# Post-norm decoder layer, experts: from all experts on all tokens to sorted blocks through one expert each, with the sorting done beside the cross attention

## The chip, the core and the metric

The kernel runs on one core of a Trainium2 chip. The metric is the time of one execution on the device, in microseconds (us); lower is better. A core has TensorE (PE in the rows; PEld is its load of stationary operands), VectorE (DVE), ScalarE (ACT), GpSimd (POOL) and SyncE (SP), which run their own instruction streams and meet at semaphores. Matrix results land in PSUM, everything else on the core lies in SBUF.

## The reference

64 sequences of 128 tokens, width 128; a context of 64 x 120 x 128. Three sublayers, each followed by `x = layernorm(x + sublayer(x))`:

```python
# 1 linear attention, 16 heads of 8, softplus features, cumulative sums over the sequence
# 2 cross attention, 16 heads of 64: latents x ask context and latents (120 + 128 keys)
q = lat @ Wq;  k, v = split(concat([layer_norm(ctx), lat]) @ Wkv)
out = softmax(q k^T / 8) v @ Wout
# 3 experts
scores = softmax(x @ gate_w.T)                     # 8 experts
topk_w, topk_i = top_k(scores, 2)
topk_w = topk_w / (topk_w.sum(-1) + 1e-20) * 2.5
g = silu(x @ w_gate[e]) * (x @ w_up[e])            # every e, F = 176
y = sum_e combine[t, e] * (g @ w_down[e])          # combine is 0 but for the two chosen
return y + (silu(x @ sw_gate) * (x @ sw_up)) @ sw_down   # shared, F = 352
```

So the two chosen of eight experts decide a token's result, and the shared part takes every token.

## The kernel before, in words

Three stages follow each other, each in a block of its own with an instruction stream per engine; everything is unrolled. `X` in SBUF (128 positions x 64 sequences x 128) carries the layer's rows from stage to stage. A product that needs more than one pass of precision is a `split_product` (L493): each operand is split into a high and a low part of type float32r, and three matmuls (hi x lo, lo x hi, hi x hi; L496, L497, L498) add up in PSUM. Transposes and the matmuls of L937 and L926 are plain float32, which the trace shows as two records each where it is a matmul and as one where it is a transpose.

**Cross attention** (`cross_attention`, L501) goes in 32 rounds of two sequences, 16 units a round; a unit `s` is two heads of one sequence. TensorE's order in unit `s` is: transpose the probabilities of unit `s` (L962), scores of unit `s+3` (L496 to L498 into `ps_S`), in even units the product `G` for a later pair, in odd ones a tile of values `V`, and every fourth unit the weighted values of four units (L937, "gang"). In unit 2 it also makes the output projection of the round before (L926). The chain of one unit is: scores, maximum (VectorE L793), exponentials (ScalarE L735), reciprocal (VectorE L799, in `inverse`), scaling of the probabilities (GpSimd L660, in `weights`), transpose (TensorE L962), copy (ScalarE L743). VectorE's order in unit `s` is `V_copy` in even units, `G_lo` (L779) in odd ones, `out_copy` in every fourth, then `maxima(s+3)` and `inverse(s+2)`. GpSimd scales unit `s+2` and puts small things between: deviation, normalisation (L652) and the copy into `X` (L655) of the round before, and key and context work. Ahead of the first round GpSimd builds a 0/1 matrix `spread`, and between the scaling of units 1 and 2 it splits the experts' and the shared gate and up weights (L703, L705).

**Experts** (`experts`, L1023) takes 16 groups of 512 tokens. The 8 x 176 expert columns and the 352 shared ones are 14 blocks of 128 (11 and 3), each a gate and an up `split_product` over 512 tokens; 11 `spread_weights` matmuls (L1332) turn the token's eight weights into a factor per expert column, and 14 `split_product`s with `down` add up `ps_y`. ScalarE makes silu (L1179) and the high part of `hidden` (L1168), VectorE the products (L1264, L1270) and the routing, 21 small operations a group (L1224 to L1247), GpSimd the low part (L1124) and the last normalisation (L1138 to L1145).

## Time and profile before

| | |
|---|---|
| median of 3 runs | 2255.25 us (2255.05 to 2255.89) |
| the profiled execution | 2259.26 us, its span 2257.3 us |
| linear attention, 0 to 311 us | not touched but for semaphore names |
| set-up of cross attention | 311 to 338.1 us |
| 32 rounds | 338.1 to 1674.6 us |
| experts | 1687.4 to 2257.3 us |
| busy share of the span | PE 96%, DVE 69%, ACT 62%, POOL 61% |
| mean granted clock of TensorE | 0.983 of full |

A row of the busy time by stage has the stretch, its length, then for PE, PEld, DVE, ACT and POOL the busy time with the number of instructions, the granted clock, the share of the DMA engines, and GB/s. TensorE's matmuls are pipelined: one takes 0.28 to 0.40 us from start to end, and the next starts before it ends, so throughput is read from the distance of the starts. In a timeline the bracket behind an instruction is the idle time of its engine before it and who ended it.

### The profile page before, as it was taken

What the parts mean: (1) busy time and instruction counts of PE and PEld (TensorE: products, weight loads), DVE (VectorE), ACT (ScalarE), POOL (GpSimd) and SP (SyncE); (2) the same over time, 40 slices, a digit from 0 to 9 for tenths busy, and PEclk for the clock granted to TensorE, in tenths of its full rate; (3) what the DMA queues carried; (4) which work ended last, traced back from release to release, by engine and by line L of the source; (5) the groups of instructions that cost most, each with busy time, mean ns of one, the idle gap of its engine ahead of it and who ended that gap; (6) DMA issues with size and microseconds to landing.
All of it is one profiled execution on the core that took longest, in us unless ns stands there. A gap on an engine that the chain in (4) does not pass through costs nothing. (4 is left out here: it accounts for less than half of the span.)

```text
span 2257.3 us, 44552 instructions
## 1 busy us (share of the span) xinstructions
PE 2164.8 (96%) x16235; PEld 1847.5 (82%) x16235; DVE 1548.4 (69%) x3425; ACT 1395.0 (62%) x3756; POOL 1372.0 (61%) x1481
## 2 busy tenths in 40 slices
PE   6899968999999999999999999999989999999998
PEld 3555547999999999999999999999977777777776
DVE  3799955666666666666666666666657777777775
ACT  3455535666666676666766666666745665665664
POOL 4688846565565665655655656656644666666666
PEclk9999979999999999999999999999999999999999
DMA  3311100000000000000000000000000000000000
GB/s 100 111 34 32 32 24 6 11 6 6 11 6 6 11 6 9 8 6 11 6 6 10 6 6 10 6 6 10 6 1 1 10 5 10 10 6 11 10 6 15
DMA packets 52794, 33.40 MB, mean 15 GB/s; under 512 B 3096, under 2 KB 50274, under 8 KB 52450
## 3 DMA queue, kind: packets, MB, share of 16 engines
q1 hardware_dynamic: 50174, 26.30, 4.0%
q10 hardware_dynamic: 2404, 4.26, 0.7%
q8 instruction: 131, 2.15, 0.4%
q14 instruction: 85, 0.70, 0.1%
HBM read 22.16 MB, written 8.39 MB: 14 GB/s over the span
## 5 line engine op out<-in xcount | busy, mean ns | idle before, releaser
L660 POOL TENSOR_TENSOR x_prob<-x_prob,x_inv 128x496 f32<-128x496 f32 x514 | 520.8, 1013 | 548.9 <-DVE x_inv L799 548.8
L735 ACT ACTIVATE x_prob<-x_ps_S,x_nmax 128x248 f32<-128x248 f32 x1028 | 473.3, 467 | 131.0 <-DVE x_nmax L793 131.0
L793 DVE TENSOR_REDUCE x_nmax<-x_ps_S 128x2 f32<-128x496 f32 x515 | 345.5, 671 | 182.8 <-PE x_ps_S L498 182.5
L743 ACT COPY x_probT<-x_ps_T 124x512 f32<-124x512 f32 x512 | 300.4, 587 | 226.3 <-PE x_ps_T L962 226.3
L1124 POOL TENSOR_TENSOR e_hidden_lo<-e_hidden,e_hidden_hi 128x512 fp32r<-128x512 f32 x224 | 291.2, 1303 | 198.4 <-ACT e_hidden_hi L1168 197.6
L496 PE MATMUL x_ps_S<-x_kT_lo,x_G_hi 128*128 128x248 f32 x1030 | 329.8, 320 | 0.0
L962 PE MATMUL x_ps_T<-ident,x_prob 128*124 128x128 f32 x2048 | 314.8, 276 | 11.7 <-POOL x_prob L660 11.7
L962 PEld LDWEIGHTS x_ps_T<-ident,x_prob 128*124 128x124 f32 x2048 | 237.6, 139 | 72.0 <-POOL x_prob L660 29.5
L497 PE MATMUL x_ps_S<-x_kT_hi,x_G_lo 128*128 128x248 f32 x1030 | 287.2, 279 | 0.0
L498 PE MATMUL x_ps_S<-x_kT_hi,x_G_hi 128*128 128x248 f32 x1030 | 286.8, 278 | 0.0
L779 DVE TENSOR_TENSOR x_G_lo<-x_ps_G,x_G_hi 128x512 fp32r<-128x512 f32 x259 | 178.8, 690 | 130.0 <-ACT x_G_hi L729 129.9
L937 PE MATMUL x_ps_O<-x_probT,x_V 124*64 124x128 f32 x4096 | 251.8, 276 | 0.2 <-ACT x_probT L743 0.2
L937 PEld LDWEIGHTS x_ps_O<-x_probT,x_V 124*64 124x64 f32 x4096 | 221.0, 137 | 18.9 <-issue 5.1
L1179 ACT ACTIVATE e_silu<-e_ps_gate 128x512 f32<-128x512 f32 x224 | 134.5, 601 | 155.7 <-PE e_ps_gate L498 150.3
L729 ACT CAST x_G_hi<-x_ps_G 128x512 fp32r<-128x512 f32 x259 | 152.0, 587 | 91.8 <-PE x_ps_G L498 91.8
L735 ACT ACTIVATION_READ_ACCUMULATOR x_prob<-x_ps_S,x_nmax 128x1 f32 x1028 | 206.5, 201 | 0.0
L497 PEld LDWEIGHTS x_ps_S<-x_kT_hi,x_G_lo 128*128 128x128 f32 x1030 | 196.4, 191 | 0.0
L496 PEld LDWEIGHTS x_ps_S<-x_kT_lo,x_G_hi 128*128 128x128 f32 x1030 | 195.6, 190 | 0.0
L498 PEld LDWEIGHTS x_ps_S<-x_kT_hi,x_G_hi 128*128 128x128 f32 x1030 | 194.9, 189 | 0.0
L1264 DVE TENSOR_TENSOR e_act_up<-e_silu,e_ps_up 128x512 f32<-128x512 f32 x176 | 120.3, 684 | 90.7 <-PE e_ps_up L498 52.7
L785 DVE COPY x_V<-x_ps_V 124x512 f32<-124x512 f32 x259 | 176.7, 682 | 2.3 <-PE x_ps_V L498 2.3
L282 POOL TENSOR_TENSOR lin_kv<-lin_qk,lin_v 128x1024 f32<-128x1024 f32 x64 | 135.1, 2129 | 32.8 <-issue 22.0
(199 smaller groups left out, 5015.4 us busy)
## 6 DMA issues: line engine op xcount, KB each, us to landing
x_nk<-latents SPq DMA_DIRECT2D x34, 124.0 KB
lin_x_rows<-in_x SPq DMA_DIRECT2D x32, 128.0 KB, 2.3
latents<-lin_nlat SPq DMA_DIRECT2D x32, 128.0 KB, 1.8
out_dram<-e_result SPq DMA_DIRECT2D x16, 256.0 KB, 2.2
x_nk<-in_ctx SPq DMA_DIRECT2D x34, 120.0 KB, 2.2
w_wkv<-in_L_xattn_Wkv SPq DMA_DIRECT2D x1, 1024.0 KB, 6.2
w_rows<-in_L_ffn_w_gate SPq DMA_DIRECT2D x1, 704.0 KB, 5.9
w_rows<-in_L_ffn_w_up SPq DMA_DIRECT2D x1, 704.0 KB, 6.2
```

Of the source, the lines that this page charges most:

```text
L496: nc.tensor.matmul(out, stationary[0], moving[1], start=first, stop=False)
L497: nc.tensor.matmul(out, stationary[1], moving[0], start=False, stop=False)
L498: return nc.tensor.matmul(out, stationary[0], moving[0], start=False, stop=last)
L660: nc.gpsimd.tensor_tensor(prob[:, k], prob[:, k], inv[:, k].unsqueeze(2).broadcast_to([P, 2, K]), ALU.mult).then_inc(prob_ready, 1)
L735: nc.scalar.activation(prob[:, k, h, :], ps_S[:, n % BANKS, h * K:(h + 1) * K], ACT.Exp, bias=nmax[:, k, h:h + 1], accum_out=total[:, k, h ...
L743: nc.scalar.copy(probT[0:KT, s % (2 * GANG)], ps_T[0:KT, s % 2, :]).then_inc(probT_ready, 1)
L779: nc.vector.tensor_tensor(G_part[1][:, pair].rearrange("p h u q -> p (h u q)"), ps_G[:], G_part[0][:, pair].bitcast(F32).rearrange("p h u ...
L785: nc.vector.tensor_copy(V[:, hf, u, tile, :], ps_V[0:KT, :]).then_inc(V_ready, 1)
L793: nc.vector.tensor_reduce(nmax[:, k, :], ps_S[:, n % BANKS, 0:2 * K].rearrange("p (h k) -> p h k", h=2), AX, ALU.max, negate=True).then_in ...
L937: last = nc.tensor.matmul(ps_O[h * DH:(h + 1) * DH, k * S:(k + 1) * S], V[:, j // 4, u, tile, (j % 4 * 2 + h) * DH:(j % 4 * 2 + h + 1) * D ...
L962: last = nc.tensor.transpose(ps_T[0:KT, s % 2, at:at + S], prob[:, s % RINGS, h, tile * KT:(tile + 1) * KT], ident[:])
L1124: nc.gpsimd.tensor_tensor(hidden_part[1][0:rows, n % RING, :], hidden[0:rows, n % 2, :], hidden_part[0][0:rows, n % RING, :].bitcast(F32), ...
```

## The change

Only the experts that a token has chosen are computed for it.

During the cross attention, each round also handles the two finished sequences of the round before: TensorE transposes their rows (`turn_rows`) and makes logits (`logits`, plain float32); VectorE works out choice, weights and place in 25 small steps (`route`), spread over units 11, 13, 14 and 15 and over units 0, 3 and 6 of the next round; TensorE counts ranks within the expert with triangular and all-ones matrices (`ranks`, 4 small matmuls) in unit 2 of the next round; GpSimd copies the rows twice into a staging buffer with their number (`keep`, `twin`) and sends both copies by four indirect DMAs (`scatter`) to the place of their expert in a DRAM array. The transposed rows go to DRAM too. The split of the expert weights moves into the units of round 0.

The experts stage then runs over 2 x 71 blocks of 128 sorted rows (16384 rows and room for an incomplete block of each expert in both halves): a block is loaded from DRAM at a row read from a table, transposed, split, taken through gate and up of one expert (one `split_product` with 352 moving columns), multiplied by its weights, transposed, taken through `down` in plain float32, and scattered by an indirect DMA to the rows' own places in a second DRAM array. Twelve row buffers are waited for in sets of three. TensorE puts the shared part of 16 groups between the blocks, eight pieces a group; two groups go ahead of the blocks. The two results of a token are loaded back, eight groups beside the second half's blocks and eight behind the last, added to `X`, and normalised. The number of an expert is read into a register of TensorE for each block, the row of a block into one of SyncE.

Its core (a line of "..." stands where lines are left out):

```diff
+BATCHES = 2
+PER = B // BATCHES
+REGION = PER * S + P
+BLOCKS = (2 * PER * S + EXPERTS * (P - 1)) // P
+SPARE = BLOCKS - 2 * PER * S // P
+BATCH_ROWS = EXPERTS * REGION + SPARE * P
+CLOSERS = BATCHES * (EXPERTS + SPARE)
+WIDTH = D + 4
...
+            def twin(n):
+
+                nc.gpsimd.tensor_copy(staged[:, n % 2, 1, :, 0:D], staged[:, n % 2, 0, :, 0:D]).then_inc(twin_ready, 1)
+                nc.gpsimd.tensor_copy(staged[:, n % 2, :, :, D].bitcast(U32), ids[:, :, n * 2:n * 2 + 2]
+                                      ).then_inc(twin_ready, 1)
+
+            def scatter(n, c, u):
+
+                pool.wait_ge(twin_ready, n * 2 + 2)
+                pool.wait_ge(routed, (n + 1) * STEPS)
+                nc.gpsimd.indirect_dma_start(slots.rows, bass.IndirectOffsetOnAxis(slot[:, n % 2, c, u:u + 1], 0),
+                                             staged[:, n % 2, c, u, :], None).then_inc(slots.scattered[n % 2], 16)
...
-                        deviation(r - 1, s - 4)
-                    if s == 6:
+                    if s in (1, 3) and r > 2:
+                        scatter(r - 3, 1, s // 2)
+                    if s == 4 and r:
+                        deviation(r - 1)
+                    if s in (5, 6) and r:
+                        normalise(r - 1, s - 5)
+                    if s > 13 and r > 1:
+                        scatter(r - 2, 0, s - 14)
+                    if s == 7:
                         keys_hi(r + 1, 1 - par)
-                    if s == 7:
+                    if s == 8:
                         keys_lo(r + 1, 1 - par)
-                    if later_round(r) and s in (8, 9):
-                        normalise(r - 1, s - 8)
-                    if s == 10:
+                    if s == 9 and r:
+                        keep(r - 1)
+                    if s == 10 and r:
+                        twin(r - 1)
+                    if s == 11:
                         context_deviation(r + 2)
-                    if s in (11, 12):
-                        normalise_context(r + 2, par, s - 11)
+                    if s in (12, 13):
+                        normalise_context(r + 2, par, s - 12)
...
+            nc.gpsimd.iota(ids[:], [[B * S, 2], [S, B]], base=0, channel_multiplier=1).then_inc(set_ready, 1)
+            nc.gpsimd.memset(ones[:].bitcast(F32), 1.0).then_inc(set_ready, 1)
+            nc.gpsimd.memset(picked[:].bitcast(F32), 0.0).then_inc(set_ready, 1)
+            for e in range(EXPERTS):
+                nc.gpsimd.memset(index[:, e:e + 1], float(e)).then_inc(set_ready, 1)
+                for n in range(BATCHES):
+                    nc.gpsimd.memset(slots.base[:, n, e:e + 1], float(n * BATCH_ROWS + e * REGION)).then_inc(set_ready, 1)
+            nc.gpsimd.tensor_tensor(before[:], tri[:], ident[:], ALU.subtract).then_inc(set_ready, 1)
             for k in range(2):
                 weights(k, k)
...
             rounds(pool, body)
+            last = ROUNDS - 1
             for u in range(2):
-                deviation(ROUNDS - 1, u)
-                normalise(ROUNDS - 1, u)
-            pool.wait_ge(part_ready, 4)
-            pool.wait_ge(spread_ready, 1)
+                scatter(last - 2, 1, u)
+            for k in range(4):
+                scatter(last - 1, k // 2, k % 2)
+            deviation(last)
+            for u in range(2):
+                normalise(last, u)
+            keep(last)
+            twin(last)
+            for k in range(4):
+                scatter(last, k // 2, k % 2)
...
+            ROUTE = {11: (0, 2), 13: (2, 6), 14: (6, 11), 15: (11, 16)}
+            ROUTE_LATE = {0: (16, 20), 3: (20, 22), 6: (22, STEPS)}
...
+            pe.wait_ge(wT_ready, 5)
+            pe.wait_ge(set_ready, SETS)
...
+            def turn_rows(n):
+
+                pe.wait_ge(staged_ready, n * 2 + 2)
+                pe.wait_ge(outT_ready, min((n + 1) * GANGS + 2, ROUNDS * GANGS))
+                for u in range(2):
+                    last = nc.tensor.transpose(ps_O[:, u * S:(u + 1) * S], staged[:, n % 2, 0, u, 0:D], ident[:])
+                last.then_inc(xT_psum, 1)
+
+            def logits(n):
+
+                pe.wait_ge(xT_ready, n + 1)
+                for u in range(2):
+                    last = nc.tensor.matmul(ps_O[:, 2 * S + u * EXPERTS:2 * S + (u + 1) * EXPERTS],
+                                            xT[:, n % 2, u * S:(u + 1) * S], gwT[:], start=True, stop=True)
+                last.then_inc(logit_psum, 1)
+
+            def ranks(n):
+
+                pe.wait_ge(routed, n * STEPS + 15)
+                pe.wait_ge(outT_ready, min((n + 2) * GANGS, ROUNDS * GANGS))
+                flat = picked[:].rearrange("p k e -> p (k e)")
+                at = 3 * S
+                nc.tensor.matmul(ps_O[:, at:at + 2 * EXPERTS], before[:], flat[:, EXPERTS:3 * EXPERTS], start=True, stop=False)
+                nc.tensor.matmul(ps_O[:, at:at + 2 * EXPERTS], ones[:], flat[:, 0:2 * EXPERTS], start=False, stop=True)
+                at += 2 * EXPERTS
+                nc.tensor.matmul(ps_O[:, at:at + EXPERTS], ones[:], flat[:, EXPERTS:2 * EXPERTS], start=True, stop=False)
+                nc.tensor.matmul(ps_O[:, at:at + EXPERTS], ones[:], flat[:, 2 * EXPERTS:3 * EXPERTS], start=False, stop=True
+                                 ).then_inc(rank_psum, 1)
...
                     if s % GANG == 0 and unit + s:
+                        if s == 12 and r:
+                            pe.wait_ge(shifted_ready, r)
+                        if s == 4 and r > 1:
+                            pe.wait_ge(routed, (r - 2) * STEPS + 22)
                         gang_output(r * GANGS + s // GANG - 1)
+                    if s == 2 and r > 1:
+                        ranks(r - 2)
 
```

The experts stage, new functions (GpSimd, VectorE, SyncE and TensorE):

```diff
+            def load_rows(q):
+
+                if q >= LOADS:
+                    sp.wait_ge(sent[(q - LOADS) % SENDS], through(q - LOADS, SENDS))
+                for i in range(q * SET, min((q + 1) * SET, TOTAL)):
+                    if i == BLOCKS:
+                        sp.wait_ge(tails_stored[1], (EXPERTS + 1) * 16)
+                    row = sp.value_load(entry(row_of, i), min_val=0, max_val=BATCHES * BATCH_ROWS - P)
+                    sp.dma_start(x_rows[:, i % RING, :], slots.rows[bass.ds(row, P), :]).then_inc(rows_loaded[q % LOADS], 16)
...
+            def scatter(i):
+
+                pool.wait_ge(y_ready, i + 1)
+                nc.gpsimd.indirect_dma_start(slots.results,
+                                             bass.IndirectOffsetOnAxis(x_rows[:, i % RING, D:D + 1].bitcast(mybir.dt.uint32), 0),
+                                             y[:, i % (SET * SENDS), :], None).then_inc(sent[i // SET % SENDS], 16)
+
+            def add_pair(g):
+
+                pool.wait_ge(back_loaded[g % BACKS], (g // BACKS + 1) * 32)
+                nc.gpsimd.tensor_tensor(back[:, g % BACKS, 0], back[:, g % BACKS, 0], back[:, g % BACKS, 1], ALU.add
+                                        ).then_inc(pair_ready, 1)
...
+            for t in range(TOTAL + 4):
+                i = t - 3
+                if 0 <= i < TOTAL:
+                    scatter(i)
+                for delay, what in ((0, add_pair), (3, deviation)):
+                    g = back_at(t, delay)
+                    if g is not None:
+                        what(g)
+            for g in range(BACK, GROUPS):
+                add_pair(g)
+                if g > BACK:
+                    deviation(g - 1)
+            deviation(GROUPS - 1)
 
...
+            sent_after(act, TOTAL)
+            for g in range(BACK, BACK + BACKS):
+                load_back(act, g)
+            for g in range(BACK, GROUPS):
+                if g + BACKS < GROUPS:
+                    load_back(act, g + BACKS)
+                normalise(g)
...
+            def take(i):
+
+                dve.wait_ge(y_psum, i + 1)
+                if i % SET == 0 and i >= SET * SENDS:
+                    q = i // SET - SENDS
+                    dve.wait_ge(sent[q % SENDS], through(q, SENDS))
+                v.tensor_copy(y[:, i % (SET * SENDS), :], ps_y[:, 0:D]).then_inc(y_ready, 1)
...
+            def gate_up(i, e):
+
+                pe.wait_ge(lo_ready, i + 1)
+                wait(pe, hidden_ready, i - 1)
+                split_product(nc, ps_gu[:, i % 2, 0:2 * F], [x[:, i % 2, :] for x in xT_part],
+                              [w[:, bass.ds(e, 1), :, :].rearrange("p o n f -> p (o n f)") for w in later.gate_up]
+                              ).then_inc(gu_psum, 1)
...
+            def project_down(i, e):
+
+                pe.wait_ge(hT_ready, i + 1)
+                wait(pe, y_ready, i)
+                for n in range(2):
+                    last = nc.tensor.matmul(ps_y[:, 0:D], hT[:, i % 2, n * P:(n + 1) * P],
+                                            later.down[:, bass.ds(e, 1), n, :].rearrange("p o d -> p (o d)"),
+                                            start=(n == 0), stop=(n == 1))
+                last.then_inc(y_psum, 1)
+
+            def shared(g, k):
+
+                if k < NS:
+                    n, rows = g * NS + k, rows_of[k]
+                    if k == 0:
+                        pe.wait_ge(all_lo_ready, g + 1)
+                    moving = [x[:, g % 2, :] for x in all_part]
+                    wait(pe, all_silu_ready, n)
+                    split_product(nc, ps_gate[0:rows, :], [w[:, k * P:k * P + rows] for w in later.shared[0]], moving
+                                  ).then_inc(gate_psum, 1)
+                    wait(pe, all_hidden_ready, n)
+                    split_product(nc, ps_up[0:rows, :], [w[:, k * P:k * P + rows] for w in later.shared[1]], moving
+                                  ).then_inc(up_psum, 1)
+                elif k < NS + GROUP:
+                    q = k - NS
+                    if q == 0:
+                        pe.wait_ge(all_hidden_ready, (g + 1) * NS)
+                        wait(pe, added, g)
+                    for n in range(NS):
                         rows = rows_of[n]
...
+            for t in range(TOTAL + 4):
+                if t < TOTAL:
+                    turn_rows(t)
+                if 0 <= t - 1 < TOTAL:
+                    gate_up(t - 1, expert[t - 1])
+                g, k = shared_at(t)
+                if g is not None:
+                    shared(g, k)
+                if t + 1 < TOTAL:
+                    expert[t + 1] = pe.value_load(entry(expert_of, t + 1), min_val=0, max_val=EXPERTS - 1)
+                if 0 <= t - 2 < TOTAL:
+                    turn_hidden(t - 2)
+                if 0 <= t - 3 < TOTAL:
+                    project_down(t - 3, expert.pop(t - 3))
 
 
```

## Rows read from the trace of the kernel before

**Rows 1.** Busy time by stage: set-up, rounds, end of cross attention, experts.
```profile
311.00:338.10 27.10, 21.30 (x100) 17.71 (x100) 13.06 (x27) 10.01 (x24) 14.15 (x17) 0.65 0.11 29
338.10:1674.60 1336.50, 1327.04 (x12608) 1236.52 (x12608) 875.72 (x2009) 898.01 (x2814) 775.27 (x956) 1.00 0.03 7
1674.60:1687.40 12.80, 5.78 (x64) 5.37 (x64) 1.88 (x6) 0.00 (x0) 4.76 (x10) 0.91 0.00 1
1687.40:2257.30 569.90, 553.71 (x2497) 435.94 (x2497) 417.99 (x931) 333.56 (x562) 362.73 (x330) 0.98 0.03 8
```

**Rows 2.** Waits from 400 to 1600 us: who waited for whom, total, times, longest.
```profile
POOL x_prob L660 <- DVE x_inv L799: 493.8, 319, 4.4
...
PEld x_ps_T L962 <- POOL x_prob L660: 15.9, 87, 0.2
```

**Rows 3.** Timeline of TensorE, part of a round: start, length, instruction.
```profile
1051.06 0.60 PE L962 MATMUL x_ps_T<-ident,x_prob 128*124 128x128 f32 x4
1051.42 0.36 PE L496 MATMUL x_ps_S<-x_kT_lo,x_G_hi 128*128 128x248 f32 x1
...
1052.19 0.28 PE L496 MATMUL x_ps_G<-x_kT_lo,x_M_hi 128*128 128x256 f32 x1
...
1052.99 1.97 PE L937 MATMUL x_ps_O<-x_probT,x_V 124*64 124x128 f32 x32
1054.89 0.66 PE L962 MATMUL x_ps_T<-ident,x_prob 128*124 128x128 f32 x4
...
1056.07 0.39 PE L496 MATMUL x_ps_V<-x_wv_lo,x_kT_hi 128*124 128x512 f32 x1
1056.30 0.39 PE L497 MATMUL x_ps_V<-x_wv_hi,x_kT_lo 128*124 128x512 f32 x1
...
1058.60 3.73 PE L926 MATMUL x_ps_V<-w_wo,x_outT 128*128 128x128 f32 x32
1062.17 0.60 PE L962 MATMUL x_ps_T<-ident,x_prob 128*124 128x128 f32 x4
```

**Rows 4.** Timeline of VectorE in the same round.
```profile
1047.60 0.69 DVE L785 COPY x_V<-x_ps_V 124x512 f32<-124x512 f32 x1
1048.73 0.68 DVE L793 TENSOR_REDUCE x_nmax<-x_ps_S 128x2 f32<-128x496 f32 x1 [0.43 <-PE x_ps_S L498]
...
1050.06 0.69 DVE L779 TENSOR_TENSOR x_G_lo<-x_ps_G,x_G_hi 128x512 fp32r<-128x512 f32 x1 [0.59 <-ACT x_G_hi L729]
```

**Rows 5.** Timeline of GpSimd in the same round.
```profile
1049.55 1.02 POOL L660 TENSOR_TENSOR x_prob<-x_prob,x_inv 128x496 f32<-128x496 f32 x1 [0.80 <-DVE x_inv L799]
1051.48 1.01 POOL L660 TENSOR_TENSOR x_prob<-x_prob,x_inv 128x496 f32<-128x496 f32 x1 [0.92 <-DVE x_inv L799]
```

**Rows 6.** Groups by line and form, 1700 to 2257 us: busy, mean ns, idle before.
```profile
L1124 POOL TENSOR_TENSOR e_hidden_lo<-e_hidden,e_hidden_hi 128x512 fp32r<-128x512 f32 x208 | 268.8, 1295 | 186.9 <-ACT e_hidden_hi L1168 186.1
...
L1179 ACT ACTIVATE e_silu<-e_ps_gate 128x512 f32<-128x512 f32 x207 | 124.4, 601 | 140.1 <-PE e_ps_gate L498 134.7
...
L1243 DVE TENSOR_TENSOR e_picked<-e_both,e_score 128x32 f32<-128x32 f32 x15 | 17.6, 1174 | 0.0
...
L1140 POOL TENSOR_TENSOR e_rstd<-e_vare,e_half 128x4 f32<-128x4 f32 x16 | 16.6, 1038 | 1.3
...
L1242 DVE TENSOR_TENSOR e_both<-e_first,e_second 128x32 f32<-128x32 f32 x15 | 2.9, 192 | 0.5
```

**Rows 7.** Timeline of TensorE: first product of values, and its longest wait.
```profile
323.97 0.79 PE L496 MATMUL x_ps_V<-x_wv_lo,x_kT_hi 128*124 128x512 f32 x1 [1.42 <-DVE x_M_lo L840]
...
351.25 1.11 PE L962 MATMUL x_ps_T<-ident,x_prob 128*124 128x128 f32 x4 [9.22 <-POOL x_prob L660]
```

**Rows 8.** Timeline behind the last round.
```profile
1677.50 3.81 PE L926 MATMUL x_ps_V<-w_wo,x_outT 128*128 128x128 f32 x32 [0.88 <-DVE x_outT L789]
...
1682.54 0.23 POOL L644 TENSOR_SCALAR x_vare<-x_mom 128x1 f32<-128x1 f32 x1 [6.87 <-DVE x_mom L812]
```

**Rows 9.** DMA issues: size, median us to landing.
```profile
out_dram<-e_result SPq DMA_DIRECT2D x16, 256.0 KB, 2.2
```

More of the change, by code:

```diff
@@ L1014, in _ @@
             output(ROUNDS - 1)
+            ranks(ROUNDS - 2)
+            pe.wait_ge(routed, (ROUNDS - 2) * STEPS + 22)
+            turn_rows(ROUNDS - 1)
+            logits(ROUNDS - 1)
+            ranks(ROUNDS - 1)
 GROUP = 4
@@ new lines, in sent_after, with load_back @@
+        def sent_after(engine, count):
+            last = (count - 1) // SET
+            for q in (last - 1, last):
+                engine.wait_ge(sent[q % SENDS], through(q, SENDS))
+        def load_back(engine, g):
+            wait(engine, sum_ready, g - BACKS + 1)
+            for c in range(2):
+                at = c * B * S + g * TOKENS
+                engine.dma_start(back[:, g % BACKS, c], slots.results[at:at + TOKENS, :].rearrange("(b s) d -> s b d", s=S)
+                                 ).then_inc(back_loaded[g % BACKS], 16)
@@ L1311, in _ @@
+            for g in range(BACK, GROUPS):
+                add_back(g)
+                if g > BACK:
+                    shifts(g - 1)
+            shifts(GROUPS - 1)
         @block.tensor
         def _(pe):
[L1313 to L1326 removed]
@@ new lines, in _ @@
+            pe.wait_ge(later.mlps_loaded, 128)
+            shared(0, 0)
+            pe.wait_ge(table_ready, TABLE - 2)
+            for n in range(2):
+                for batch in range(BATCHES):
+                    at = (n * BATCHES + batch) * P
+                    last = nc.tensor.transpose(ps_y[0:1, at:at + P], place[:, n, batch:batch + 1], ident[:])
+            last.then_inc(table_psum, 1)
+            for g in range(EARLY):
+                for k in range(PIECES):
+                    if g + k:
+                        shared(g, k)
```

918 lines of the change are left out of this document (552 added, 366 removed).

## The prediction

> **What bounds the kernel now.** I read the busy time by stage first. In the 32 rounds TensorE is busy 1327.0 of 1336.5 us, in the experts 553.7 of 569.9, at the full clock or nearly (1.00 and 0.98); the others are busy at most 67% and 73% [rows 1]. The waits confirm it: from 400 to 1600 us the load of TensorE's operands waits for GpSimd 15.9 us in all, never over 0.2 at a time, while GpSimd waits 493.8 us for its inputs [rows 2]. So both stages go at TensorE's pace, and what counts is TensorE's work, and whether another engine becomes late enough to hold it. A round takes 1336.5/32 = 41.8 us.
>
> Prices of TensorE, from distances of starts [rows 3]: a float32 transpose (1051.42 - 1051.06)/4 = 0.09; a product with 248 columns (1052.19 - 1051.42)/6 = 0.13; with 512 columns 0.23; so with 352 about 0.17. A float32 matmul is two records: L926 puts 32 in 3.57 us, so 0.22 a matmul; L937 32 in 1.90, 0.12.
>
> **Experts, the work.** A block costs TensorE 1 transpose (0.09), 3 x 0.17 = 0.51, 2 transposes (0.18), 2 float32 matmuls (0.44): 1.22 us. A shared group costs 18 x 0.23 + 12 x 0.22 = 6.8 us. Before, a group was 137 products and 3 for the logits at 0.23 and some 16 transposes, 33.7 us, and the stage took 569.9/16 = 35.6 [rows 1], a factor of 1.06, which I take over for gaps.
> - Head: the first shared rows have to land (2.2 [rows 9]) and be split (about 0.6 and 0.7, by the 0.60 that ScalarE takes for 512 columns [rows 6]), 4 us; then two shared groups ahead of the blocks, one gate and one up buffer, 15 us. Regions are closed, the table is made and the first rows loaded beside it. 19 us.
> - 112 iterations with shared work: 14 x (8 x 1.22 + 6.8) x 1.06 = 14 x 17.6 = 246 us. ScalarE has three instructions of 128 to 256 columns a block, an estimated 1.0 us at half to two thirds of the 0.60; it fits.
> - 34 iterations without it (30 blocks and the drain): GpSimd scatters a block (price S, below), and every seven iterations adds a pair and makes a deviation, 1.30 + 1.04 + 0.23 = 2.6 us [rows 6, 8], 0.37 each. With S = 1.2 that is 1.57 against TensorE's 1.22: 53 us.
> - Tail: the last scatter lands (2.2), a load (2.2), then eight groups at GpSimd's 2.6 = 21, last normalisation and store about 4: 30 us.
>
> Sum 348 us against 569.9: 222 us less.
>
> **What no row prices.** S, an indirect DMA on GpSimd: below, 0.23, its smallest instruction here [rows 8]; above, 2.2, if it held the engine until a transfer has landed [rows 9]. 128 addresses worked out in software are nearest to an instruction that works through a tile, 1.0 to 1.3 [rows 5, 6]; I take 1.2. At 2.2 the sum rises by 34 in those iterations, 8 behind the rounds and 9 in them, 51 us. By the Trainium skill, page "DMA: Bandwidth & Descriptors", section "Latency and other measured facts", a DMA from GpSimd has its first byte after about 1 us, for the work of writing descriptors; as S that would make the experts 7 us shorter by estimate; no run here shows it. The reading of a register on TensorE, 142 times: from nothing, if queued matmuls cover it (in 112 cases shared products are queued ahead of it), to about 1.0 us, GpSimd's 1.01 for a whole tile [rows 5], in the 34 others, 34 us. I take nothing and keep the rest for the range.
>
> **Cross attention, per round.** TensorE gets 2 transposes (0.18), 2 float32 matmuls for the logits (0.44 by L926, 0.24 by L937) and 4 small matmuls for the ranks (up to 0.13 each, held by their operand loads): 0.7 to 1.1 us, all on the path, since nothing there is idle. I take 1.1, as L926 loads operands of the same 128 x 128.
>
> VectorE gets 25 small operations of about 0.2 (L1242, [rows 6]). They stand behind `inverse`, so what queues behind them is the next unit's `V_copy` or `G_lo`, the next maximum, and through it the exponentials, the scaling on GpSimd and the transpose. Places with slack: the reciprocal of unit 16 (that is, unit 0 of the next round) leads to a scaling that ends at 1050.57, and its transpose starts at 1051.06: 0.49 us [rows 3, 5]. The next scaling ends at 1052.49 and is used at 1054.89: 2.4 us. `G_lo` ends at 1050.75 and is needed behind the scores, at 1052.19: 1.4 us [rows 3, 4].
>
> Two-input operations on VectorE have a second price: L1243 takes 1174 ns and L1242 with the same shapes 192 [rows 6]. Four of the 20 routing steps are such; GpSimd was then in its 1.3 us instruction. So a cluster of route steps beside a scaling of 1.01 us waits up to once, about 0.95. Unit 13: 4 x 0.2 + 0.95 = 1.8, less 0.43 idle before the maximum [rows 4], 1.4 late, less 0.49 slack: 0.9 us on TensorE. Units 14 and 15: 5 steps each, 1.95 us each, against slack of 1.4 to 2.4 and the 0.9 by which TensorE has moved: about 0.5. The clusters at 11, 0, 3 and 6 stand before the weighted values, the output projection (3.57 us) or with over 2 us of slack, and I cost them at nothing; without that cover each would cost up to 1. Together 1.4.
> The Trainium skill, page "SBUF — State Buffer", section "Who interferes with whom", says that a VectorE instruction with two SBUF inputs contends with a GpSimd instruction that reads SBUF. The 1174 against 192 ns agree. Without such waits the 1.4 us would go and the sum be 43 us lower.
>
> GpSimd gets 4 scatters, `keep` and `twin`. In unit 14 it sat idle 0.92 us before its next scaling [rows 5], so S = 1.2 is 0.3 late, 0.8 after the second, against 2.4 of slack: nothing. At S = 2.2 it would be some 0.3 a round. The clusters' waits for `shifted` and `routed` ahead of the weighted values are met by then, as the logits are three TensorE units or the ranks 4 us ahead.
>
> 31 rounds x (1.1 + 1.4) = 78 us.
>
> **Start and end of cross attention.** TensorE now waits for GpSimd's set-up (29 increments; about 3 us of memsets behind its context work, which ends near 327.5) before its first product of values at 323.97: 7 us later. The 9.22 us that it waited at 351.25 for the weight splits [rows 7] go; they come back spread over ten units of round 0, some 12 us of GpSimd work against more than that idle, 3 us. Net +1.
> Behind the last round (output from 1677.50 [rows 8], next stage at 1687.40 [rows 1]) the routing of the last sequences is bare: 9 steps of the round before (2 us), 4 scatters (4.8), deviation and normalisation (4), transpose, copy, logits (2), 16 steps and the exponential (4), ranks and 5 steps (1.5), 4 scatters (4.8): 23 us from 1683, 1706 instead of 1687.4: +19.
>
> **Sum.** 2257.3 - 222 + 78 + 1 + 19 = 2133 us of span. The profiled execution took 2259.26 and the median of the runs is 2255.25, 2 us below the span: **2131 us**.
>
> **Rivals.**
> - *The cover holds everywhere* (no VectorE stalls, logits at 0.12): 78 becomes 31 x 0.7 = 22, S = 0.23 takes another 15, a gap factor of 1.00 instead of 1.06 another 14: 2046, and below 2035 if the tail overlaps better than its 30 us. For: the slack of 2.4 us. Against: 0.49.
> - *VectorE and GpSimd block each other twice per cluster*: 3 x 0.95 more in each round, 31 x 2.9 = 90, about 2220. For: 1174 ns. Against: GpSimd idles between scalings.
> - *The other side: the pace of a block is set outside TensorE*, by the scatter or by the loop scatter, `sent`, `load_rows`, transposition. The gain of 124 us over 146 iterations is 0.85 a piece above today's sum of 299/146 = 2.05: from 2.9 us an iteration (S above 2.5) on, the kernel is not faster; at 3.5, with 146 x 1.45 = 212 us more, it takes 2340. For: no indirect transfer is in the trace, and GpSimd must build each. Against: 2.2 us to land, while the ring gives 12 blocks. The Trainium skill, page "SBUF — State Buffer", section "SBUF: two separate sides", has a GpSimd DMA starved by a VectorE copy from SBUF to SBUF, 620 ns turned into 3100; as S that would be this rival by estimate. The wide copies on VectorE here read PSUM, so I give it no more weight.
> - *It does nothing*: gain and loss meet within 0.2% (4.5 us, about what a measurement can tell here).
>
> **Chances.** Forecast and its surroundings (2035 to 2210) 0.66; cover holds, below 2035, 0.07; blocking, 2210 to 2250, 0.13; no change 0.02; slow blocks 0.12. Faster 0.86, same 0.02, slower 0.12. Leaving out the lowest 0.07 and the slow blocks gives 2035 to 2245.
>
> **What would show it.** A round of 44.3 us instead of 41.8, TensorE's waits for L660 in units 0 and 1; GpSimd's time between a scatter and its next instruction (1.2); iterations of 2.2 us with shared work and 1.6 without; a tail of about 30 us without TensorE; some 23 us between the last projection and the experts. Wrong would make it an S above 2.5, register reads that stop TensorE, or a lower granted clock where TensorE waits for blocks.

## The result, and the profile after

The changed kernel takes 2202.7 us (median of 4 runs, 2201.88 to 2205.46), the kernel before 2255.57 in the same comparison: ratio 0.9763, 95% interval 0.9748 to 0.9777. So it is 53 us faster, where 124 were forecast; 2131 was 72 us too low, inside its range of 2035 to 2245. The profiled execution of the changed kernel took 2202.96 us with a span of 2201.2.

Busy time by stage of the changed kernel, in the columns of [rows 1]; the borders of stages are its own:

```profile
311.00:346.00 35.00, 20.66 (x101) 17.14 (x101) 13.16 (x28) 11.54 (x28) 10.28 (x41) 0.63 0.09 26
346.00:1751.00 1405.00, 1381.89 (x12930) 1271.30 (x12932) 1070.74 (x2769) 908.72 (x2877) 890.40 (x1049) 1.00 0.05 16
1751.00:1784.80 33.80, 7.97 (x68) 7.12 (x64) 9.54 (x48) 0.59 (x2) 15.21 (x20) 0.64 0.09 28
1784.80:2201.20 416.40, 327.44 (x2096) 271.02 (x2096) 218.55 (x684) 185.79 (x555) 191.94 (x208) 0.92 0.33 92
```

The first three stages came out as forecast, to within 2.5 us each. In the rounds the pace is best read from the residual, one addition a round:

```profile
L922 DVE TENSOR_TENSOR x_hsum<-x_ps_V,X x32: 423/424/424, 396.2 to 1757.8; 128x256 f32<-128x256 f32 x32
```

From the first to the last are 31 rounds in 1361.6 us; before, the same row reads 397.7 to 1681.3, 1283.6 us. That is 78.0 us more, the 78 of the forecast. The first lies 1.5 us earlier (+1 was forecast). From the last to the start of the experts it is now 27.0 us (before, 1681.3 to 1687.4, 6.1): +21 against +19.

So the miss is in the experts: 416.4 us where 348 were forecast, 68 us. Here is the stage cut at block 0, at block 112 (the last with shared work is 111) and at the end of the last scatter:

```profile
1784.80:1809.40 24.60, 18.29 (x89) 12.82 (x89) 10.79 (x27) 6.10 (x9) 5.32 (x18) 0.81 0.30 83
1809.40:2088.70 279.30, 256.06 (x1691) 217.82 (x1690) 149.69 (x441) 132.29 (x405) 121.35 (x121) 0.99 0.29 82
2088.70:2156.60 67.90, 53.09 (x321) 40.37 (x319) 37.60 (x136) 34.23 (x110) 44.96 (x46) 0.97 0.35 101
2156.60:2201.20 44.60, 0.00 (x0) 0.00 (x0) 20.47 (x80) 13.17 (x32) 20.30 (x25) 0.50 0.50 143
```

| part | forecast | measured | miss |
|---|---|---|---|
| head | 19 | 24.6 | 5.6 |
| 112 iterations with shared work | 246 | 279.3 | 33.3 |
| 34 without it | 53 | 67.9 | 14.9 |
| tail | 30 | 44.6 | 14.6 |

Four places in the trace stand out. The first is at the first blocks (timeline of TensorE):

```profile
1809.40 0.27 PE L1742 MATMUL e_ps_x<-ident,e_x_rows 128*128 128x128 f32 x1
1817.83 0.79 PE L517 MATMUL e_ps_gate<-e_all_lo,w_shared_gate_hi 128*128 128x512 f32 x1 [8.16 <-DVE e_all_lo L1626]
```

The split of shared group 2 is late because its rows are: on SyncE their load is queued behind twelve row loads of 1.12 us each.

```profile
1800.26 13.46 SPq L1410 DMA_DIRECT2D e_x_rows<-sorted_rows  x12
1813.77 1.86 SPq L1399 DMA_DIRECT2D e_all_xT<-turned_rows  x4
```

Within a group of shared work, whose eight iterations take 19.0 us where 17.6 were forecast, TensorE stands once for the last hidden values:

```profile
1922.03 0.94 PE L1791 MATMUL e_ps_s<-w_shared_down,e_all_hidden 128*128 128x128 f32 x6 [0.55 <-DVE e_all_hidden L1636]
```

In the last iterations (VectorE, then the TensorE row that waits), one block's subtraction stands behind VectorE's whole part of the way back:

```profile
2104.91 0.69 DVE L1650 TENSOR_TENSOR e_hsum<-e_back,X 128x512 f32<-128x512 f32 x1 [1.23 <-POOL e_back L1499]
2105.63 0.87 DVE L1654 BATCH_NORM_STATS2 e_stat<-e_hsum 128x6 f32<-128x128 f32 x4
2106.54 0.38 DVE L1657 BATCH_NORM_AGGREGATE e_mom<-e_stat 128x2 f32<-128x6 f32 x4
2106.84 0.26 DVE L1605 TENSOR_TENSOR e_xT_lo<-e_ps_x,e_xT_hi 128x128 fp32r<-128x128 f32 x1
```

```profile
2107.24 0.30 PE L1742 MATMUL e_ps_x<-ident,e_x_rows 128*128 128x128 f32 x1 [2.20 <-DVE e_xT_lo L1605]
```

And in the tail a group comes every 4.64 us (all engines, part of one):

```profile
2174.12 1.26 POOL L1499 TENSOR_TENSOR e_back<-e_back 128x512 f32<-128x512 f32 x1
2174.47 1.46 DVE L1650 TENSOR_TENSOR e_hsum<-e_back,X 128x512 f32<-128x512 f32 x1 [1.81 <-ACT e_result L1565]
...
2177.16 0.13 DVE L1662 SCALAR_TENSOR_TENSOR e_shift<-e_mom,e_rstd 128x4 f32<-128x4 f32 x1
2177.33 0.49 ACT L1565 ACTIVATE e_result<-e_hsum,e_shift,e_rstd 128x128 f32<-128x128 f32 x1 [2.99 <-DVE e_shift L1662]
...
2178.11 0.86 ACT L1565 ACTIVATE e_result<-e_hsum,e_shift,e_rstd 128x128 f32<-128x128 f32 x2
2178.76 1.26 POOL L1499 TENSOR_TENSOR e_back<-e_back 128x512 f32<-128x512 f32 x1
2179.11 1.46 DVE L1650 TENSOR_TENSOR e_hsum<-e_back,X 128x512 f32<-128x512 f32 x1 [1.81 <-ACT e_result L1565]
```

The addition waits until two groups back is normalised (`hsum` has two buffers), and the next shift, which ScalarE needs, is queued behind that addition: one closed loop over VectorE and ScalarE.

### The profile page after: what moved, and what is told of

Read it like the earlier page. It is cut to its first block and busy times, and to the rows that moved or that the text cites. A ratio compares the mean times of both kernels' runs of the same rounds, so it can differ in the third digit from the quotient of the medians.

```text
span 2201.2 us, 47735 instructions
## 1 busy us (share of the span) xinstructions
PE 1994.3 (91%) x16155; PEld 1718.1 (78%) x16155; DVE 1551.4 (70%) x3978; ACT 1258.4 (57%) x3814; POOL 1322.8 (60%) x1485
## 5 line engine op out<-in xcount | busy, mean ns | idle before, releaser
L1492 POOL DMA_INDIRECT sorted_results<-e_y,e_x_rows x142 | 145.8, 1026 | 198.8 <-DVE e_y L1621 189.3
L721 POOL DMA_INDIRECT sorted_rows<-w_rows,x_slot x128 | 132.0, 1032 | 36.1 <-issue 22.8
L517 PE MATMUL x_ps_G<-x_kT_lo,x_M_hi 128*128 128x256 f32 x518 | 149.6, 289 | 0.2 <-DVE x_G_lo L896 0.2
```

The source lines that it names most:

```text
L517: nc.tensor.matmul(out, stationary[0], moving[1], start=first, stop=False)
```

## The experiments

Every kernel was timed against the kernel before. A thousandth of the ratio is 2.3 us; the changed kernel has 0.9763. e5, e7 and e8 don't compute the layer's output; they only tell times.

| kernel | us | ratio, 95% interval |
|---|---|---|
| e1, three buffers for the sums | 2191.9 | 0.9711 (0.9695 to 0.9727) |
| e2, shared rows first | 2193.9 | 0.9718 (0.9701 to 0.9735) |
| e3, rows constant | 2195.7 | 0.9724 (0.9708 to 0.9740) |
| e4, expert constant | 2196.1 | 0.9729 (0.9712 to 0.9745) |
| e5, plain store | 2201.0 | 0.9751 (0.9735 to 0.9767) |
| e6, e2 and 18 row buffers | 2194.8 | 0.9724 (0.9708 to 0.9740) |
| e7, no routing steps | 2147.9 | 0.9522 (0.9506 to 0.9538) |
| e8, e7 without logits and ranks | 2125.9 | 0.9421 (0.9405 to 0.9437) |
| e9, e1 and e2 | 2183.3 | 0.9675 (0.9661 to 0.9688) |
| e10, e9, sum later | 2180.9 | 0.9668 (0.9654 to 0.9681) |
| e11, e10, moments apart | 2173.0 | 0.9637 (0.9624 to 0.9650) |
| e12, e11, normalisation apart | 2171.1 | 0.9626 (0.9613 to 0.9639) |
| e13, e12, down projection later | 2164.9 | 0.9597 (0.9583 to 0.9610) |
| e14, e13 and 18 row buffers | 2158.8 | 0.9566 (0.9553 to 0.9579) |

**e1, the tail's loop opened.**

```
-        hsum = room.sbuf("hsum", [P, 2, GROUP, D])        # mom, rstd, shift too
+        hsum = room.sbuf("hsum", [P, HELD, GROUP, D])     # HELD = 3
-                wait(dve, result_ready, (g - 1) * GROUP)
+                wait(dve, result_ready, (g - HELD + 1) * GROUP)
```

> The changed kernel takes 2202.7 us. Theory: behind the last block the eight groups go at 4.64 us each because group g's addition on VectorE waits for group g-2 to be normalised on ScalarE, and the next shift is queued behind that addition: 1.65 (normalise) + 1.46 (addition) + 0.87 + 0.38 (statistics) + 0.13 (shift) = 4.5 in one loop. With hsum, mom, rstd and shift held in three buffers the loop opens, and VectorE's 2.84 or GpSimd's 2.8 a group is next: 7 x 1.7 = 12 us less, 2191. Rival: GpSimd's pair addition and VectorE's addition slow each other so that the pair of them is the pace with or without the wait: within 3 us of 2202.7.

11 us less, as the theory had it. VectorE's additions in its tail, two of them:

```profile
2172.65 0.69 DVE L1651 TENSOR_TENSOR e_hsum<-e_back,X 128x512 f32<-128x512 f32 x1
...
2175.51 0.69 DVE L1651 TENSOR_TENSOR e_hsum<-e_back,X 128x512 f32<-128x512 f32 x1
```

2.86 us a group instead of 4.64, and from the last block's transposition to the end 41.4 us instead of 51.4. The addition takes 0.69 instead of 1.46; in the kernel before this edit each of the five long ones (1.27 to 1.46) started inside GpSimd's addition of a pair, and here none does.

**e2, the order on SyncE.**

```
+            load_all(2)
             for q in range(LOADS):
                 load_rows(q)
-            load_all(2)
             load_all(3)
```

> Theory: block 1 starts 11.2 us behind block 0 because TensorE waits 8.2 us for the split of shared group 2, whose rows stand on SyncE behind twelve row loads of 1.12 us each. Its loads are now ahead of them: 6 to 8 us less, 2195 to 2197. Rival: the row loads, 1.9 us later, or what follows them on SyncE hold the blocks instead: at most 2 us less.

9 us less, slightly over the theory's 6 to 8. Block 1 starts at 1811.43, 1.5 us behind block 0 at 1809.92, where it was 11.2. e9 holds both edits and takes 2183.3: 19.4 us less than the changed kernel, where the two alone give 10.8 and 8.8, so they add up.

> Three held buffers and the shared rows first together. They act behind the last block and ahead of the first ones, so they should add: 2202.7 - 11.3 - 9.5 = 2182, within 2 us. Rival: the tail's gain was partly time that the earlier end gives back: 2186 or more.

**e3 and e4, without register reads.**

```
-                    row = sp.value_load(entry(row_of, i), ...)
+                    row = ROWS_AT[i]
```
```
-                    expert[t + 1] = pe.value_load(entry(expert_of, t + 1), ...)
+                    expert[t + 1] = EXPERT_AT[t + 1]
```

> The 142 starts of row blocks are constants (those of this input), so SyncE reads no register for them; the closing of regions keeps its reads. Theory: SyncE's 1.12 us a row load is mostly the register read (the loads of turned rows without it take 0.46); SyncE's queue paces the start (12 x 0.66 = 8 us less before shared group 2) and part of the last 60 iterations: 10 to 20 us less, 2183 to 2193. Rival: the last iterations wait for the round trip scatter, landing, row load, landing, not for SyncE's issuing: only the start's 8 us go, 2195. Second rival: the read costs nothing, 2203.

> The 142 expert numbers are constants (those of this input), so TensorE reads no register and its weights have fixed addresses. The prediction took the read as nothing, with up to 1.0 us in each of 34 iterations as its bound. Theory after the trace: the products of a block without shared work stand 0.2 to 0.3 us apart where TensorE shows no wait; 30 x 0.3 to 0.5 = 9 to 15 us less, 2188 to 2194. Rival one, nothing: 2203. Rival two, the bound: about 2170.

e3 gains 7 us, the first rival's number. On SyncE the twelve row loads now take

```profile
1800.83 5.56 SPq L1411 DMA_DIRECT2D e_x_rows<-sorted_rows  x12
```

0.46 each instead of 1.12, so the read costs 0.66. The distance of blocks 0 and 1 falls from 11.2 to 2.9 us, and nothing else does: blocks 112 to 141 take 61.8 us against 61.0. It is the same stall as in e2, removed in another way; SyncE's issuing sets no pace later.

e4 gains 7 us, less than the theory's 9 to 15, and in another place: the 112 iterations take 274.2 instead of 279.3, the last 29 60.3 instead of 61.0. Where shared products are queued around it, a read with its addresses costs TensorE 5.1/112 = 0.05 us. In the last 29 iterations it costs more than the total shows. Waits of the operand load and of TensorE there, in the changed kernel and then in e4:

```profile
PEld e_ps_h L1758 <- issue: 11.4, 27, 0.9
PE e_ps_x L1742 <- DVE e_xT_lo L1605: 8.2, 8, 2.2
```

```profile
PE e_ps_x L1743 <- DVE e_xT_lo L1606: 13.9, 8, 3.1
```

The first of these stands where the read does, between a block's gate and up products and the transposition of `hidden`, and it is gone in e4. An iteration that nothing else holds falls from 1.60 to 1.26 us, so the read costs 0.34 there:

```profile
2092.33 0.28 PE L1743 MATMUL e_ps_x<-ident,e_x_rows 128*128 128x128 f32 x1
...
2093.59 0.28 PE L1743 MATMUL e_ps_x<-ident,e_x_rows 128*128 128x128 f32 x1
```

The total hardly moves, as TensorE now waits longer for VectorE (13.9 us instead of 8.2), and its granted clock in this stretch is 0.86 on average instead of 0.97.

**e5 and e6, the scatter and the ring.**

```
-                nc.gpsimd.indirect_dma_start(slots.results, bass.IndirectOffsetOnAxis(...), y[...], None)
+                nc.gpsimd.dma_start(slots.results[i * P:(i + 1) * P, :], y[...])
```
```
-    LOADS = 4
+    LOADS = 6
```

> A block's results go with a plain DMA from GpSimd's queue to rows that follow each other, so the output is not the reference's; the same 142 stores of 64 KB, and the sorting during cross attention stays. Theory: a scatter holds GpSimd 0.96 us and 0.30 behind it, and its landing 3.7 us after its start stands in the ring's round trip. With 0.3 us instead the 30 last iterations go at TensorE's pace of 1.65 instead of 2.1: about 12 us less, 2191, and at most 3 more from the iterations with shared work. Rival: the row loads and their landing behind 256 KB transfers hold the blocks whatever the store is: within 4 us of 2202.7.

> On the kernel that loads shared rows first (2193.9), eighteen row buffers in six sets instead of twelve in four. Theory: the last 29 iterations take 2.1 us each because block n's rows are requested when block n-12's set has landed in the results: 110's scatter starts at 2094.8, its landing is seen at 2098.5, the loads take until 2107.0, and block 120 waits for them. Six blocks more of slack: those iterations fall to 1.65 us, 12 us less, 2182. Rival: GpSimd's own sum (1.26 a scatter and 2.6 in seven iterations, 1.63) or SyncE's order keeps the pace, and nothing moves: within 3 us of 2193.9.

Both theories fell. The plain store holds GpSimd 0.54 us instead of 0.96 and leaves the last 29 iterations at 61.0 us, as before; with 18 buffers they take 63.1 (62.1 in e2). In e6, TensorE still stands every seventh iteration, and for the same row as before:

```profile
2099.63 0.30 PE L1745 MATMUL e_ps_x<-ident,e_x_rows 128*128 128x128 f32 x1 [2.19 <-DVE e_xT_lo L1608]
...
2114.79 0.45 PE L1745 MATMUL e_ps_x<-ident,e_x_rows 128*128 128x128 f32 x1 [1.48 <-DVE e_xT_lo L1608]
...
2130.24 0.30 PE L1745 MATMUL e_ps_x<-ident,e_x_rows 128*128 128x128 f32 x1 [2.34 <-DVE e_xT_lo L1608]
```

15.2 and 15.5 us apart: the period of a group on its way back. The wait is for VectorE, as the row says. e6's theory had put it down to the row loads, because they landed just then. That made the next theory.

**e10, e11 and e12, the way back taken apart.**

```
-                g = back_at(t, 1)          # e10: add_back 3, deviation 5, shifts 7,
+                g = back_at(t, 3)          # normalise 8, store 3 iterations behind
                 if g is not None:
                     add_back(g)
```
```
+                g = back_at(t, 4)          # e11: the bn_stats of add_back
+                if g is not None:
+                    moments(g)
+                g = back_at(t, 5)          # and its bn_aggr, in functions of their own
+                if g is not None:
+                    aggregate(g)
```
```
+                for k in range(GROUP):     # e12
+                    g = back_at(t, 8 + k)
+                    if g is not None:
+                        normalise(g, (k,))
```

> On the one before: the sum with the pair stands three iterations behind the pair's addition on GpSimd instead of one (deviation, shift, normalisation and store move back by two or three with it). New theory, since neither ring nor scatter moved anything: every seven iterations VectorE's part of the way back (wait for the pair 1.2, addition 1.46, statistics 0.87 and 0.38) stands between two blocks' subtractions, and TensorE waits 2.2 us for the second of them. Without the wait for the pair, and with the addition at 0.7 when GpSimd isn't in its own, 1.2 to 2.0 us less eight times: 2168 to 2173. Rival: the stall comes from the shift's wait for GpSimd's deviation or from ScalarE's four normalisations in a row: within 3 us of the run before.

> On the one before: addition, statistics and their aggregation in three successive iterations instead of one. By the new theory what is left of the stall (0.87 + 0.38 behind the addition, against some 0.5 us of slack in an iteration of 1.65) goes: 8 x 0.7 = 6 us less than the run before. Rival: TensorE's slack already covers it, nothing less.

> On the one before: ScalarE's four normalisations (1.65 us in a row) go one in each of four iterations. ScalarE has about 1.0 us of block work in an iteration of 1.65, so four in a row make the next block's copy about 1 us late: 8 x 0.5 to 1.0 = 4 to 8 us less. Rival: the copy has that slack: nothing less.

e10 gains 2.3 us with overlapping intervals, not 10 to 15: the wait of TensorE falls from 2.2 to 0.9 us, but the last 29 iterations only from 60.9 to 59.2. Its expectation took the one long wait for the whole loss, and it counted the addition at the tail's 1.46 us, where it takes 0.69 here already (2104.91 in the rows of the result). e11 gains 8 more, over its 6. By the profiled executions 6.5 of them lie where the edit acts: the last 29 iterations take 54.7 us, 4.5 less, and the 32 before them 2.0 less. VectorE's pieces of a group now stand each between two blocks' own work:

```profile
2093.36 0.68 DVE L1654 TENSOR_TENSOR e_hsum<-e_back,X 128x512 f32<-128x512 f32 x1
2093.96 0.28 DVE L1609 TENSOR_TENSOR e_xT_lo<-e_ps_x,e_xT_hi 128x128 fp32r<-128x128 f32 x1
...
2094.67 0.86 DVE L1661 BATCH_NORM_STATS2 e_stat<-e_hsum 128x6 f32<-128x128 f32 x4
2095.45 0.27 DVE L1609 TENSOR_TENSOR e_xT_lo<-e_ps_x,e_xT_hi 128x128 fp32r<-128x128 f32 x1
```

So most of the loss was that addition, statistics and aggregation stood in one piece. e12 gives nothing that can be measured (0.9637 and 0.9626 with overlapping intervals): ScalarE had the slack.

**e13, the group's down projection one iteration later.**

```
-                elif k < NS + GROUP:
-                    q = k - NS
+                elif k > NS:
+                    q = k - NS - 1
```

> On the run before (2171.1): the four pieces of a shared group's down projection stand in iterations 4 to 7 of eight instead of 3 to 6, so that an iteration lies between the last gate and up piece and the first of them. Theory: a group of eight iterations takes 19.05 us where 17.6 were predicted; TensorE stands 0.55 to 0.9 us at the third of them for VectorE's last product of hidden values, and 0.27 at the next one. That goes, 14 times 0.9: 12 us less, 2159. Rival: the wait is only moved to the next use of what VectorE makes (its queue is late for the block's own subtraction too), or the excess is the block's own 1.27 to 1.45 us on TensorE against the 1.22 predicted: at most 3 us less.

Eight iterations fall from 19.05 to 18.0 us and the 112 from 266.8 to 253.0, 13.8 less and so the theory's 12. But the whole gains 6: the last 29 go from 54.0 to 58.5. The longest wait of TensorE there is this one, and e14's theory takes it for the row loads:

```profile
2074.49 0.45 PE L1761 MATMUL e_ps_x<-ident,e_x_rows 128*128 128x128 f32 x1 [1.77 <-DVE e_xT_lo L1610]
```

It isn't theirs. VectorE's subtraction stands behind a shift that waits 2.60 us for GpSimd's `rstd`, and the same wait is in e11 (1.78) and e12 (1.76), before this edit:

```profile
2073.98 0.16 DVE L1673 SCALAR_TENSOR_TENSOR e_shift<-e_mom,e_rstd 128x4 f32<-128x4 f32 x1 [2.60 <-POOL e_rstd L1514]
```

**e14, 18 buffers again.** The edit of e6 on e13.

> On the run before (2164.9): eighteen row buffers again. With twelve they moved nothing (e6), where VectorE's part of the way back held TensorE. The iterations with shared work now take 18.0 us in eight, but the 29 iterations behind them went from 54.0 to 58.5 us. Theory: the blocks come sooner now and the rows' round trip is next to hold them (TensorE stands 1.8 us before a transposition at 2074.5): with six more buffers those iterations come back to 54 or less, 2159. Rival: GpSimd's own sum (1.26 a scatter, 2.6 in seven iterations: 1.63 each, and a backlog from the iterations before) sets them: nothing less.

The 29 iterations come back to 53.4 us, and the whole gains 6. The wait that the theory started from stays as it was:

```profile
2075.71 0.30 PE L1761 MATMUL e_ps_x<-ident,e_x_rows 128*128 128x128 f32 x1 [1.77 <-DVE e_xT_lo L1610]
```

What goes is elsewhere: block 115's iteration falls from 2.68 to 1.64 us, those of blocks 129 to 131 from 7.4 to 5.1. No row of e13 names the row loads there, but the edit does nothing other than give them more slack. So the round trip of the rows over DRAM does hold blocks once VectorE doesn't, shown by the edit and not by a wait in the trace. The same edit was worth nothing in e6. This is the fastest version that computes the layer, 0.9566 of the kernel before and 44 us below the changed one.

**e7 and e8, what the rounds paid.**

```
                 for k in range(first_k, end_k):
+                    if k not in (18, 19):
+                        continue
```
```
-                    last = nc.tensor.matmul(ps_O[:, 2 * S + u * EXPERTS:...], xT[...], gwT[:], ...)     # e8
-                nc.tensor.matmul(ps_O[:, at:at + 2 * EXPERTS], before[:], flat[...], ...)       # and three more
```

> Of VectorE's 25 routing steps a round only the two that write the weights stay (from constants); the places are a table made once, each expert gets 1024 rows of each half, so the output is not the reference's. TensorE's turning, logits and ranks, ScalarE's exponential and all scatters stay, and the number of blocks too. The prediction had 1.4 of a round's 2.5 us more as TensorE's waits behind VectorE's steps, and 4 + 1.5 + 2 us of bare steps behind the last round. By it: 31 x 1.4 + 7 = 50 us less, 2152. Rival one: a round's 2.5 us are TensorE's own work and its gaps: 7 us less, 2195. Rival two: the waits come from the scatters on GpSimd, which stay: 10 to 15 less, 2190.

> As the one before, and TensorE's two logit products and four rank products a round are left out too. The prediction had 0.24 to 0.44 for the logits and up to 0.5 for the ranks: 31 x 0.9 = 28 us and about 1 us behind the rounds less than the run before, 2123 if that one gives 2152. Rival: they fit into gaps that TensorE has anyway: nothing less than the run before.

The residual's rows of e7, then of e8:

```profile
L925 DVE TENSOR_TENSOR x_hsum<-x_ps_V,X x32: 424/425/426, 394.1 to 1707.2; 128x256 f32<-128x256 f32 x32
```

```profile
L925 DVE TENSOR_TENSOR x_hsum<-x_ps_V,X x32: 424/425/426, 393.8 to 1682.7; 128x256 f32<-128x256 f32 x32
```

1313.1 and 1288.9 us for 31 rounds, after 1361.6 with everything and 1283.6 before the change. A round's 2.5 us are 48.5/31 = 1.56 for VectorE's steps, 24.2/31 = 0.78 for logits and ranks, and 5.3/31 = 0.17 for all else (turning, scatters). The forecast said 1.4 for the first, 0.92 for the second (of its 1.1, the rest being the transposes), and 0.18 for the third. Behind the last round e7 goes from 27.0 to 18.7 us, 8.3 less where 7 were expected.

## Why the prediction was right about cross attention and wrong about the experts

- **Rounds, 78 us: right in sum and in kind, half wrong in place.** VectorE's steps cost 1.56 us a round where 1.4 were forecast, TensorE's own work 0.95 where 1.1 were. The contention that it took from L1243 and L1242 [rows 6] is there in small: `chosen`, 128 x 16 with two inputs, takes 1.03 us beside GpSimd's scaling, and `rest`, next to it, 0.18:

```profile
1043.06 1.03 DVE L1000 TENSOR_TENSOR x_chosen<-x_order,x_col 128x16 f32<-128x16 f32 x1
1044.12 0.18 DVE L1002 SCALAR_TENSOR_TENSOR x_rest<-x_chosen,x_score 128x16 f32<-128x16 f32 x1
```

 By the Trainium skill, page "SBUF — State Buffer", section "Who interferes with whom", that is what a VectorE instruction with two SBUF inputs meets beside a GpSimd instruction that reads SBUF; the trace agrees.

 The place was only half right. The forecast had 0.9 us at the transposition behind unit 13, 0.5 behind units 14 and 15, and nothing for the cluster at 0. The operand loads show where TensorE waited from 400 to 1600 us (27 rounds), in the changed kernel and then in e7:

```profile
PEld x_ps_T L1200 <- POOL x_prob L745: 21.4, 53, 0.6
PEld x_ps_V L1131 <- DVE x_V L902: 19.1, 27, 0.7
```

```profile
PEld x_ps_T L1198 <- POOL x_prob L746: 0.3, 2, 0.2
```

 In one round of the changed kernel:

```profile
1044.10 0.41 PEld L1200 LDWEIGHTS x_ps_T<-ident,x_prob 128*124 128x124 f32 x4 [0.63 <-POOL x_prob L745]
...
1052.56 3.65 PEld L1131 LDWEIGHTS x_ps_V<-w_wo,x_outT 128*128 128x128 f32 x32 [0.71 <-DVE x_V L902]
```

 So 0.63 us stand behind unit 13, no long wait behind units 14 and 15, and 0.71 at the output projection, where I had nothing. VectorE has no idle time there from 1039.59 to 1053.16: the clusters at 13, 14, 15 and 0 pile up, and slack counted for each by itself was not there for the last. That an overestimate of 0.8 and an omission of 0.7 meet is luck; that the total of both came near is why the 78 us did.

- **S = 1.2 us: right.** The groups of scatters on the page, in the experts and in the rounds:

```profile
L1492 POOL DMA_INDIRECT sorted_results<-e_y,e_x_rows x142 | 145.8, 1026 | 198.8 <-DVE e_y L1621 189.3
...
L721 POOL DMA_INDIRECT sorted_rows<-w_rows,x_slot x128 | 132.0, 1032 | 36.1 <-issue 22.8
```

 With 0.30 us behind a scatter of 0.96, two in a row start 1.26 us apart. In e5 this price held nobody, but VectorE's part of the way back stood in front there; on e14 the plain store was not tried. The Trainium skill, page "DMA: Bandwidth & Descriptors", section "Latency and other measured facts", has about 1 us to the first byte, for the writing of descriptors. The 1.03 lies near it; no run here shows the first byte itself.
- **Register reads on TensorE as nothing: nearly right beside shared work, wrong without it.** They cost 0.05 us each in the 112 iterations (e4). In the others they cost 0.34, which e4's total hides. The condition that I had named, shared products queued ahead, was the right one.
- **Head and the first of the 112 iterations: wrong, about 15 us.** "Regions are closed, the table is made and the first rows loaded beside it" costed SyncE's queue at nothing. It asks for shared group 2 only behind twelve loads of 1.12 us: 9 us, shown by e2, and by e3 from the other side. The other 6 lie ahead of block 0, where two shared groups took 20.3 us instead of 15. Each of them by itself:

```profile
1789.05:1800.53 11.48, 10.34 (x47) 7.20 (x47) 5.43 (x16) 3.17 (x5) 1.21 (x2) 0.77 0.30 88
1800.53:1809.40 8.87, 7.95 (x46) 5.59 (x44) 2.75 (x4) 1.79 (x3) 0.00 (x0) 1.00 0.24 57
```

 The first began, after 13.3 us without work on TensorE, at a granted clock of 0.50, the lower of its two levels (1.2 GHz), and had full clock from 1795 on. The second had full clock throughout and still took 8.9 us where I had 7.5, 0.84 of them in a wait for its last hidden values. So the clock accounts for at most 2.6 us, and gaps in each group for 2.8. Neither was tested.
- **112 iterations at 17.6 us for eight: the step that failed is the factor 1.06 for gaps**, taken over from another loop. A shared group is 6.8 us as forecast; but a group's down projection follows its last hidden values in the next iteration, 1.0 us in each (e13: 13.8 us). Against the work of 16.6 us the measured 19.0 are a factor of 1.15. The 0.4 us that remain above 17.6 are the block itself: 1.27 us of TensorE's time where I had 1.22 (1925.67 to 1927.60 less the 0.66 of a shared piece). From block 80 on eight take 20.3, as the way back begins (5 us in all).
- **34 iterations at 1.57: the term that failed is the 0.37 for the way back.** I summed GpSimd (1.2 + 0.37) against TensorE (1.22) and never queued VectorE's 0.69 + 0.87 + 0.38 us and its wait of 1.2, in front of a subtraction that TensorE needs. That was 7 us (e10 to e12). The forecast's own pace, 1.57, no version reached: it is 1.84 in e14. What is left there stays open. Two paces lie next to each other: TensorE's undisturbed iteration takes 1.60 with the register read, and GpSimd's own sum is 1.63 by e14's expectation. Neither the read nor the scatter was taken out of e14.
- **Tail at 2.6 us a group: wrong, 14.6 us**, from the same omission: GpSimd alone was summed, and the loop over VectorE and ScalarE, which takes 4.64 us a group, was not drawn. e1 returns 11.
- **Rivals.** The cover did not hold (VectorE's steps cost 1.56 us a round), and VectorE and GpSimd did not block each other twice per cluster (that would have been 4.3). "The pace of a block is set outside TensorE" was right for the last blocks as a kind, but not by the scatter and only in small part by the ring; at 2.1 us it stayed under its limit of 2.9.

## What to carry to other kernels

Cost an added stage by drawing every engine's queue in it, not the busiest engine's sum: the 78 us in the old, full pipeline came out since each engine's slack was read there (in sum; slack counted place by place still missed a pile-up), and the 348 us of the new one missed by 68, above all since one engine's busy time stood for the loop. A second engine's work of 2 us in one piece, in a pipeline of 1.6 us steps, costs even at half load: give it out over several steps. And a fix that is worth nothing (18 buffers, e6) can be worth 6 us when the wait in front of it is gone (e14), so test it again. The same holds for a cost that seems to be nothing: e4's reads looked free in the last iterations only because TensorE then waited longer for VectorE.

## What the runs showed of the hardware

- A load on SyncE whose address is read from a register took 1.12 us to issue, one with a constant address 0.46 (e3).
- On TensorE a register read with its addresses cost 0.05 us an iteration beside queued shared products, and 0.34 where a block had TensorE to itself (1.60 us an iteration, 1.26 with constants, e4).
- An indirect DMA of 128 rows on GpSimd took 0.96 us and 0.30 behind it, a plain DMA of the same 64 KB 0.54 (e5).
- VectorE's addition of two SBUF tiles of 128 x 512 took 0.69 us alone, 1.27 to 1.46 when it started inside GpSimd's addition of the same size. GpSimd's own 1.26 stayed as it was.
